# Index scores with ScalarE weighing a head in every second unit, and the row statistics of the second and fourth layernorm at the ends of the attentions

## The chip, the cores and the metric

The kernel runs on one core of one Trainium2 chip, as one launch. The core has TensorE (PE in the profile: matmuls and transposes), VectorE (DVE), ScalarE (ACT), GpSimd (POOL) and SyncE (SP, which issues most DMAs). Each works through its own list of instructions in order, and they meet by semaphores. SBUF holds the tensors, 128 partitions wide; PSUM holds the matmul results in 8 banks of 512 fp32 columns. The metric is the device time of the launch in microseconds.

## What is computed

One block of a model with 2048 tokens of width 256: x goes through a layernorm and attention A, a layernorm and a mixture of experts, a layernorm and attention B, a layernorm and the same experts again. Attention A has a mask made of index scores, which is where the first part of the change lies:

```python
x = x + attn_a(layernorm(x)); x = x + ffn(layernorm(x))
x = x + attn_b(layernorm(x)); x = x + ffn(layernorm(x))

# the index scores in attn_a, HI = 4 heads of DI = 64
dots = relu(einsum('bqhd,bkhd->bhqk', qi, ki))
index_scores = einsum('bhqk,h->bqk', dots, idx_w)
thr = the adaptive_k-th largest of each row of index_scores
top_k_mask = index_scores >= thr

def layernorm(x, eps=1e-5):
    m = mean(x, -1); v = var(x, -1)
    return (x - m) / sqrt(v + eps)
```

## The kernel before

**Stages.** The program is a row of blocks with a barrier of all engines at each block's end: ln1, preparation of the index, then for each half of the queries (group, g = 0 and 1) the index scores and the threshold search, preparation of A, attention A, ln2, experts, ln3, preparation of B, attention B, ln4, experts. Between the barrier of one stage and the first work of the next, GpSimd clears semaphores. The order inside a stage is written out by hand, for each engine a list.

**Index scores** (`index_scores`). A group has 8 tiles of 128 queries, and each tile two halves of 1024 keys: 16 units. A unit has four heads. For a head TensorE makes 128x1024 dot products by four matmuls into one of four pairs of PSUM banks (L454), ScalarE takes the relu into `relu[:, h, :]` in SBUF (L477; in the profile this tile is called `x`, as its area is shared), and VectorE weighs and adds it into `scores`: the first head by a multiplication (L499), the other three by a fused multiply and add (L502). There is one relu buffer a head, so that the relu of unit u waits until VectorE has used that of unit u - 1 (semaphore `summed`), and TensorE's matmuls of unit u wait for the relu of unit u - 1 (`relu_done`). The queries of the second 512 columns are projected in between: after heads number 5, 10, 15 and 20 of the 64 (table `LATER`), TensorE makes a projection (L430), ScalarE keeps its high part (L467) and VectorE its low part (L487).

**Layernorm** (`layernorm`). VectorE takes sixteen row statistics of x, one for each tile of 128 rows (L147, in a loop of four times four), then eight small instructions on 128x16, ScalarE a square root (its function table is loaded at the block's start), VectorE a reciprocal, and then it normalizes tile after tile (L168), TensorE transposes each (L217) and ScalarE stores it (L183). ln2 and ln4 also make the router's logits (L200), which wait for the router's seven loads, issued by SP at the block's start. ln3 gets its statistics ready made: in the experts VectorE takes them (L2371) right behind the last additions to x.

**End of attention A** (`attention_a`). GpSimd adds each head's output to x (L1239), the last pair for tile 15. VectorE's last work there is splitting transposed probabilities (L1425).

**End of attention B** (`attention_b`). For each tile VectorE takes the reciprocal of 16 sums (L1916), multiplies (L1925), TensorE transposes (L1832), ScalarE stores (L1887), TensorE multiplies with the output weights (L1807), and VectorE adds the result to x (L1919), five tiles behind the products (`LATE` = 5).

Of the kernel before, what the change touches and what calls it, by code (L numbers as in the profile page):

```python
# [11 lines left out]
ALU = mybir.AluOpType  # L12
# [369 lines left out]
def index_scores(nc, tag, g, xT, psum, w_q, b_q, q_stack, k_stack, k_lo, q_alone, relu, weight, scores, high, low):  # L382
# [4 lines left out]
    UNITS = GT * HALVES  # L387
    LATER = {HI * (1 + j) + j + 1: HI + j for j in range(HI * (QC - 1))}

    def pair(h):  # L390
        return psum[:, h * WIDE:(h + 1) * WIDE]

    with Phase(nc, tag) as phase:
# [9 lines left out]
        summed = sem("summed")  # L403
        with nc.Block() as block:
# [58 lines left out]
            def _(act):  # L463
# [8 lines left out]
                for u in range(UNITS):  # L472
                    for h in range(HI):
                        act.wait_ge(dotted, u * HI + h + 1)
                        if u:
                            act.wait_ge(summed, (u - 1) * HI + h + 1)
                        nc.scalar.activation(relu[:, h, :], pair(h), ACT.Relu).then_inc(relu_done, 1)  # L477
                        if u * HI + h in LATER:
                            keep_high(LATER[u * HI + h])

            @block.vector
            def _(dve):
# [10 lines left out]
                for u in range(UNITS):  # L493
                    t, half = divmod(u, HALVES)
                    into = scores[:, t, half * WIDE:(half + 1) * WIDE]
                    for h in range(HI):
                        dve.wait_ge(relu_done, u * HI + h + 1)
                        if h == 0:
                            nc.vector.tensor_scalar(into, relu[:, h, :], weight[:, 0:1], None, ALU.mult).then_inc(summed, 1)  # L499
                        else:  # L500
                            dve.wait_ge(summed, u * HI + h)
                            nc.vector.scalar_tensor_tensor(out=into, in0=relu[:, h, :], scalar=weight[:, h:h + 1], in1=into,  # L502
# [609 lines left out]
def attention_a(nc, arg, x, xT, bank, const, k_hi, k_lo, c_stack, bias, w_out, nowhere, q_rows):  # L1112
# [15 lines left out]
    with Phase(nc, "aa") as phase:  # L1128
# [60 lines left out]
        with nc.Block() as block:  # L1189
# [211 lines left out]
            def _(dve):  # L1401
# [50 lines left out]
                walk(dve, before, run, dve_order)  # L1452

# [153 lines left out]
def attention_b(nc, arg, x, xT, psum, bank, const, stash, q_stack, k_stack, zeroed, staged, stashed, same_in, after, halves, values):  # L1607
# [51 lines left out]
    with Phase(nc, "ab") as phase:  # L1659
# [9 lines left out]
        inv = [sb(f"inv{p}", [P, HB, 1]) for p in range(DEEP)]  # L1669
# [26 lines left out]
        with nc.Block() as block:  # L1696
# [194 lines left out]
            def _(dve):  # L1891
# [21 lines left out]
                for t in range(NT + LATE):  # L1913
                    p = t % DEEP
                    if t < NT:
                        nc.vector.reciprocal(inv[p][:], o_sums[:, t, :, DHB:]).then_inc(inv_done, 1)  # L1916
                    if t >= LATE:
# [3 lines left out]
                    if t < NT:  # L1921
                        dve.wait_ge(inv_done, t + 1)
# [651 lines left out]
```

## Time and profile before

| | us |
|---|---|
| median of three timed runs | 2668.33 (2663.47 to 2684.12) |
| the profiled execution's own time | 2662.5 |
| its span, first to last instruction | 2660.6 |
| TensorE busy | 2288.9 (86%) |
| VectorE busy | 1791.9 (67%) |
| ScalarE busy | 1673.3 (63%) |
| GpSimd busy | 723.1 (27%) |
| 128 relus of the index scores (L477) | 125.1 |
| 16 + 16 row statistics of ln2 and ln4 | 5.33 and 5.32 |

Busy shares are averages over stages with different limits. In the timeline a row is one instruction or several equal ones in a row (x3), with its start, the time from the first start to the last end, its engine and line, what it writes and reads, and in brackets how long the engine stood idle ahead of it and what ended that. Instructions of one engine can overlap by a little. SPq is SP's DMA issue. "PEq L98" as a releaser is a barrier.

### The profile page before, as it was taken

The page shows a single profiled execution, that of the slowest core. Times are in us where ns is not written, and L with a number is a line of the kernel's source. Part 1 is how long each engine was busy: PE and PEld are TensorE (multiplying, and loading weights), DVE is VectorE, ACT ScalarE, POOL GpSimd, SP SyncE. Part 2 cuts the span into 40 slices and gives each one's busy share as a digit, 9 for nine tenths or more (in the row PEclk, how much of TensorE's full clock was granted, in tenths as well). Part 3 has the DMA queues.
Part 4 walks back from the last instruction along what each step waited for, and adds up shares of the span by engine and source line. Part 5 has one row for each costly group of instructions (what it writes and reads, how often), then busy time and mean ns, then how long its engine had stood idle before and what let it go on. Part 6 is the DMA issues. An engine that isn't in the chain of part 4 may idle for free. (4 is left out here: it accounts for less than half of the span.)

```text
span 2660.6 us, 41889 instructions
## 1 busy us (share of the span) xinstructions
PE 2288.9 (86%) x12536; PEld 1556.2 (58%) x12536; DVE 1791.9 (67%) x3724; ACT 1673.3 (63%) x3045; POOL 723.1 (27%) x992
## 2 busy tenths in 40 slices
PE   6956595568999999999999999799569999997995
PEld 3633363347878787877787788465335444434663
DVE  4888798875777677767776777532568778744523
ACT  3779587946777777777777777323217777774232
POOL 0215411543321432143225422046220000100163
PEclk9978797878999999999999999899769999998998
DMA  1011102131000000000000000412360101000124
GB/s 50 1 40 63 64 1 74 56 127 44 21 13 13 22 21 13 13 26 17 13 13 25 17 1 1 128 58 84 97 195 1 49 2 49 2 1 4 52 88 142
DMA packets 77559, 113.14 MB, mean 43 GB/s; under 512 B 23860, under 2 KB 51860, under 8 KB 74644
## 3 DMA queue, kind: packets, MB, share of 16 engines
q1 hardware_dynamic: 66776, 89.55, 10.7%
q0 software_dynamic: 10560, 20.86, 2.6%
q8 instruction: 110, 1.80, 0.3%
q14 instruction: 113, 0.93, 0.1%
HBM read 67.25 MB, written 39.58 MB: 40 GB/s over the span
## 5 line engine op out<-in xcount | busy, mean ns | idle before, releaser
L1425 DVE TENSOR_TENSOR aa_pt_lo<-psum,aa_pt_hi 128x512 fp32r<-128x512 f32 x544 | 350.4, 685 | 82.8 <-ACT aa_pt_hi L1355 80.2
L1899 DVE TENSOR_REDUCE ab_part_max<-psum 128x2 f32<-128x1024 f32 (+3 forms) x320 | 327.0, 1062 | 93.9 <-PE psum L1745 92.0
L1355 ACT ACTIVATE aa_pt_hi<-psum 128x512 fp32r<-128x512 f32 x544 | 297.7, 598 | 116.0 <-PE psum L1285 113.1
L1847 ACT ACTIVATE ab_prob<-psum 128x512 f32<-128x512 f32 (+3 forms) x640 | 296.9, 541 | 100.3 <-PE psum L1774 96.5
L1412 DVE CUSTOM_DVE_ANT_0 aa_prob<-psum,bias 128x512 f32<-128x512 f32 (+2 forms) x480 | 278.6, 598 | 117.2 <-PE psum L1275 98.1
L1239 POOL TENSOR_TENSOR x<-aa_y_out,x 128x256 f32<-128x256 f32 x256 | 188.7, 737 | 353.0 <-ACT aa_y_out L1373 308.4
L1273 PE MATMUL psum<-ka_hi,aa_q_hi 128*128 128x512 f32 (+3 forms) x640 | 268.0, 419 | 10.8 <-POOL aa_q_lo L1207 8.0
L1285 PE MATMUL psum<-ident,aa_prob 128*128 128x128 f32 x1600 | 252.9, 274 | 6.8 <-issue 5.4
L1347 ACT ACTIVATE aa_prob<-aa_prob,aa_neg_max 128x128 f32<-128x128 f32 (+11 forms) x192 | 228.0, 1189 | 44.0 <-DVE aa_neg_max L1418 42.4
L1774 PE MATMUL psum<-b_q_stack,b_k_stack 64*128 64x512 f32 (+3 forms) x640 | 229.4, 432 | 15.3 <-ACT ab_prob L1847 10.7
L1296 PE MATMUL psum<-aa_pt_hi,c_stack 128*128 128x512 f32 x544 | 233.6, 429 | 5.9 <-ACT aa_out_t L1362 4.3
L1275 PE MATMUL psum<-ka_hi,aa_q_lo 128*128 128x512 f32 (+3 forms) x640 | 236.4, 369 | 0.0
L1274 PE MATMUL psum<-ka_lo,aa_q_hi 128*128 128x512 f32 (+3 forms) x640 | 236.0, 369 | 0.0
L1745 PE MATMUL psum<-b_k_stack,b_q_stack 63*128 63x512 f32 (+3 forms) x640 | 226.8, 468 | 6.7 <-DVE ab_part_max L1899 6.4
L1298 PE MATMUL psum<-aa_pt_lo,c_stack 128*64 128x512 f32 x544 | 215.4, 396 | 0.0
L1285 PEld LDWEIGHTS psum<-ident,aa_prob 128*128 128x128 f32 x1600 | 193.8, 141 | 30.2 <-issue 8.2
L1774 PEld LDWEIGHTS psum<-b_q_stack,b_k_stack 64*128 64x128 f32 x640 | 112.0, 189 | 107.8 <-ACT ab_prob L1847 91.3
L1207 POOL TENSOR_TENSOR aa_q_lo<-aa_q_row,aa_q_hi 128x512 fp32r<-128x512 f32 x64 | 82.6, 1291 | 332.5 <-ACT aa_q_hi L1339 332.5
L699 PE MATMUL psum<-ixt_w_heads,xT 128*128 128x512 f32 x256 | 133.9, 674 | 23.0 <-ACT ixt_w_heads L618 23.0
L1273 PEld LDWEIGHTS psum<-ka_hi,aa_q_hi 128*128 128x128 f32 x640 | 123.3, 193 | 49.1 <-DVE aa_chunk_max L1412 17.7
L1786 PE MATMUL psum<-ab_prob,b_values 128*17 128x512 f32 (+3 forms) x1280 | 149.7, 540 | 0.0
L1308 PE MATMUL psum<-wa_out,aa_out_t 128*128 (+1 forms) x512 | 135.3, 387 | 8.3 <-ACT aa_y_out L1373 4.3
(346 smaller groups left out, 4753.3 us busy)
## 6 DMA issues: line engine op xcount, KB each, us to landing
q_rows<-ixt_q_out SPq DMA_DIRECT2D x64, 256.0 KB, 2.0
aa_q_row<-q_rows SPq DMA_DIRECT2D x64, 256.0 KB, 2.6
f_back<-done SPq DMA_DIRECT2D x16, 512.0 KB, 8.0
w<-in_w SPq DMA_DIRECT2D x6, 896.0 KB, 9.6
x<-in_hidden SPq DMA_DIRECT2D x2, 2048.0 KB, 11.3
b_q_stack<-stash_q_hi SPq DMA_DIRECT2D x12, 256.0 KB, 4.2
b_k_stack<-stash_k_hi SPq DMA_DIRECT2D x12, 256.0 KB, 4.7
ixt_wq_n<-in_Wq_nope_T SPq DMA_DIRECT2D x2, 1024.0 KB, 5.3
```

The costliest lines, as they stand in the source:

```text
L1273: nc.tensor.matmul(out[:, 0:w], q_hi[t % 2][:, head], k_hi[:, cols], start=True, stop=False)
L1274: nc.tensor.matmul(out[:, 0:w], q_hi[t % 2][:, head], k_lo[:, cols], start=False, stop=False)
L1275: nc.tensor.matmul(out[:, 0:w], q_lo[t % 2][:, head], k_hi[:, cols], start=False, stop=True).then_inc(scores_ready, 1)
L1285: last = nc.tensor.transpose(turn_bank[(TB[t] + j) % RING][:, h * P:(h + 1) * P], prob[t % 2][h][:, j * P:(j + 1) * P], const["ident"][:])
L1296: nc.tensor.matmul(out[:], c_stack[:, j, :], pt_hi[ring][:], start=j == 0, stop=j == t, skip_group_check=True)
L1347: nc.scalar.activation(prob[t % 2][h][:, 0:L], prob[t % 2][h][:, 0:L], ACT.Exp, bias=neg_max[t % SUMS][:, h:h + 1], accum_out=total[t % SU ...
L1355: nc.scalar.activation(pt_hi[(TB[t] + j) % RING][:], turn_bank[(TB[t] + j) % RING], ACT.Copy).then_inc(pt_hi_done, 1)
L1412: nc.vector.tensor_tensor_reduce(prob[t % 2][h][:, c * CH:c * CH + w], score_bank[(QB[t] + h * chunks[t] + c) % 2][:, 0:w], bias[:, TRI[t] ...
L1425: nc.vector.tensor_tensor(pt_lo[ring][:], turn_bank[(TB[t] + j) % RING], pt_hi[ring][:].bitcast(F32), ALU.subtract).then_inc(pt_lo_done, 1)
L1774: nc.tensor.matmul(out[:, 0:w], k[at, kb * P:(kb + 1) * P], q[at, q0:q0 + w], start=not diag, stop=True, skip_group_check=True).then_inc(t ...
L1847: nc.scalar.activation(prob[i % 2][h][:, 0:w], t_bank[slot % RING][:, 0:w], ACT.Exp).then_inc(t_taken, 1)
L1899: nc.vector.tensor_reduce(part_max[e % 2][:, at:at + 5:4, part], s_pair[pair % 2][:, :, 0:w], AX.X, ALU.max).then_inc(s_used, 1)
```

## The change

**Index scores.** In units with an odd number ScalarE weighs the first head: behind the relu of head 1 it writes `relu[:, 0, :]` times the weight into `scores` (a Copy with a pointer scale) and increments a new semaphore `weighed`. VectorE has no L499 in these units; its first L502 waits for `weighed`. In even units all is as before. The relu of head 0 in an even unit waits for `weighed` and not for VectorE, and the counts of `summed` are those of VectorE's 7 instructions a pair.

**Layernorms 2 and 4.** The tile `stats` is allocated at the program's start. VectorE takes the sixteen row statistics at the end of attention A, each behind GpSimd's last addition to that tile, and at the end of attention B inside the loop over tiles, one tile behind the addition. ln2 and ln4 get `stats` and leave theirs out. In attention B one reciprocal of all 256 sums, in place, stands ahead of the loop and takes the place of the sixteen.

```diff
+    DVE_SUMS = 2 * HI - 1
+        def sums(u, h):
+            return DVE_SUMS * (u // 2) + (HI if u % 2 else 1) + h
...
                         act.wait_ge(dotted, u * HI + h + 1)
-                        if u:
-                            act.wait_ge(summed, (u - 1) * HI + h + 1)
+                        if u % 2 == 0 and u and h == 0:
+                            act.wait_ge(weighed, u // 2)
+                        elif u:
+                            act.wait_ge(summed, sums(u - 1, h))
                         nc.scalar.activation(relu[:, h, :], pair(h), ACT.Relu).then_inc(relu_done, 1)
+                        if u % 2 and h == 1:
+                            act.wait_ge(relu_done, u * HI + 1)
+                            nc.scalar.activation(into(u), relu[:, 0, :], ACT.Copy, scale=weight[:, 0:1]).then_inc(weighed, 1)
...
-                        dve.wait_ge(relu_done, u * HI + h + 1)
                         if h == 0:
-                            nc.vector.tensor_scalar(into, relu[:, h, :], weight[:, 0:1], None, ALU.mult).then_inc(summed, 1)
+                            if u % 2 == 0:
+                                dve.wait_ge(relu_done, u * HI + 1)
+                                nc.vector.tensor_scalar(into(u), relu[:, 0, :], weight[:, 0:1], None, ALU.mult).then_inc(summed, 1)
                         else:
-                            dve.wait_ge(summed, u * HI + h)
+                            dve.wait_ge(relu_done, u * HI + h + 1)
+                            if u % 2 and h == 1:
+                                dve.wait_ge(weighed, u // 2 + 1)
+                            else:
+                                dve.wait_ge(summed, sums(u, h - 1))
...
                 walk(dve, before, run, dve_order)
+                for t in range(NT):
+                    dve.wait_ge(x_added, ((NG - 1) * NT + t + 1) * GH + 4 * GH)
+                    nc.vector.bn_stats(stats[:, t, :], x[:, t, :])
...
                 dve.wait_ge(t_taken, SLOTS_USED)
-                for t in range(NT + LATE):
+                nc.vector.reciprocal(o_sums[:, :, :, DHB:], o_sums[:, :, :, DHB:]).then_inc(inv_done, 1)
+                dve.wait_ge(inv_done, 1)
+                for t in range(NT + LATE + 1):
                     p = t % DEEP
-                    if t < NT:
-                        nc.vector.reciprocal(inv[p][:], o_sums[:, t, :, DHB:]).then_inc(inv_done, 1)
-                    if t >= LATE:
+                    if LATE <= t < NT + LATE:
                         dve.wait_ge(out_done, t - LATE + 1)
                         nc.vector.tensor_tensor(x[:, t - LATE, :], x[:, t - LATE, :], out_bank[(t - LATE) % DEEP][:, 0:D],
                                                 ALU.add).then_inc(x_done, 1)
                     if t < NT:
-                        dve.wait_ge(inv_done, t + 1)
                         if t >= DEEP:
                             dve.wait_ge(o_turned, t - DEEP + 1)
                         nc.vector.tensor_tensor(o[p].rearrange("p (h d) -> p h d", d=DHB), o_sums[:, t, :, 0:DHB],
-                                                inv[p][:].to_broadcast([P, HB, DHB]), ALU.mult).then_inc(o_done, 1)
+                                                o_sums[:, t, :, DHB:].to_broadcast([P, HB, DHB]), ALU.mult).then_inc(o_done, 1)
+                    if t > LATE:
+                        dve.wait_ge(x_done, t - LATE)
+                        nc.vector.bn_stats(stats[:, t - LATE - 1, :], x[:, t - LATE - 1, :])
```

ScalarE's list at the start of the index scores before (L467 keeps a projection, L477 is a relu):

```order
L467 ACTIVATE ix_q_stack<-psum,ix_b_q 128x512 x4
L477 ACTIVATE x<-psum 128x1024 x6
L467 ACTIVATE ix_q_stack<-psum,ix_b_q 128x512
L477 ACTIVATE x<-psum 128x1024 x5
L467 ACTIVATE ix_q_stack<-psum,ix_b_q 128x512
L477 ACTIVATE x<-psum 128x1024 x5
L467 ACTIVATE ix_q_stack<-psum,ix_b_q 128x512
L477 ACTIVATE x<-psum 128x1024 x5
L467 ACTIVATE ix_q_stack<-psum,ix_b_q 128x512
L477 ACTIVATE x<-psum 128x1024 x43
```

and with the change (line numbers of the changed kernel: L477 keeps a projection, L489 is a relu, L492 the new copy):

```order
L477 ACTIVATE ix_q_stack<-psum,ix_b_q 128x512 x4
L489 ACTIVATE x<-psum 128x1024 x6
L492 ACTIVATE ix_scores<-x,ix_weight 128x1024
L477 ACTIVATE ix_q_stack<-psum,ix_b_q 128x512
L489 ACTIVATE x<-psum 128x1024 x5
L477 ACTIVATE ix_q_stack<-psum,ix_b_q 128x512
L489 ACTIVATE x<-psum 128x1024 x3
L492 ACTIVATE ix_scores<-x,ix_weight 128x1024
L489 ACTIVATE x<-psum 128x1024 x2
L477 ACTIVATE ix_q_stack<-psum,ix_b_q 128x512
L489 ACTIVATE x<-psum 128x1024 x5
L477 ACTIVATE ix_q_stack<-psum,ix_b_q 128x512
```

The first copy (unit 1) stands directly ahead of the keeping of a projection, the second and third (units 3 and 5) ahead of further relus.

VectorE's list around the end of attention A and the start of ln2 before (the loop has four statistics; the first stands here):

```order
L1433 RECIPROCAL aa_inv<-aa_total 128x4
L1425 TENSOR_TENSOR aa_pt_lo<-psum,aa_pt_hi 128x512 x22
L1189 UNCONDITIONAL_BRANCH
L141 UNCONDITIONAL_BRANCH
L144 UNCONDITIONAL_BRANCH
L144 ISA
L147 ISA
L147 BN_STATS ln_stats<-x 128x6
L147 ISA
```

and with the change:

```order
L1451 RECIPROCAL aa_inv<-aa_total 128x4
L1443 TENSOR_TENSOR aa_pt_lo<-psum,aa_pt_hi 128x512 x22
L1473 BN_STATS stats<-x 128x6 x16
L1207 UNCONDITIONAL_BRANCH
L141 UNCONDITIONAL_BRANCH
L151 TENSOR_TENSOR row_mean<-stats 128x16
L152 TENSOR_TENSOR ln_half<-stats 128x16
L153 TENSOR_TENSOR ln_var<-stats 128x16
L155 TENSOR_SCALAR row_mean<-row_mean 128x16
L156 TENSOR_SCALAR ln_half<-ln_half 128x16
```

The sixteen row statistics stand ahead of the end of the attention's block (its branch) now, and ln2 starts without the loop L144.

VectorE's list at the end of attention B before, from the reciprocal of the fourth tile on:

```order
L1916 RECIPROCAL ab_inv<-ab_o_sums 128x16
L1925 TENSOR_TENSOR xT<-ab_o_sums,ab_inv 128x256
L1916 RECIPROCAL ab_inv<-ab_o_sums 128x16
L1925 TENSOR_TENSOR xT<-ab_o_sums,ab_inv 128x256
L1916 RECIPROCAL ab_inv<-ab_o_sums 128x16
L1919 TENSOR_TENSOR x<-x,psum 128x256
L1925 TENSOR_TENSOR xT<-ab_o_sums,ab_inv 128x256
L1916 RECIPROCAL ab_inv<-ab_o_sums 128x16
L1919 TENSOR_TENSOR x<-x,psum 128x256
```

and with the change, from the start of that part:

```order
L1933 RECIPROCAL ab_o_sums<-ab_o_sums 128x256
L1944 TENSOR_TENSOR xT<-ab_o_sums 128x256 x5
L1939 TENSOR_TENSOR x<-x,psum 128x256
L1944 TENSOR_TENSOR xT<-ab_o_sums 128x256
L1939 TENSOR_TENSOR x<-x,psum 128x256
L1944 TENSOR_TENSOR xT<-ab_o_sums 128x256
L1948 BN_STATS stats<-x 128x6
L1939 TENSOR_TENSOR x<-x,psum 128x256
L1944 TENSOR_TENSOR xT<-ab_o_sums 128x256
L1948 BN_STATS stats<-x 128x6
```

The reciprocals of 16 columns are gone from between the products, one of 256 columns stands ahead, and a row statistic follows each addition to x by a product.

## Rows read from the trace of the kernel before

**Rows 1.** busy time by stretch, index stage: us, PE, PEld, DVE, ACT, POOL, clock

```profile
105.00:145.00 40.00, 37.63 (x144) 24.68 (x142) 37.50 (x33) 33.50 (x34) 6.33 (x7) 1.00 0.00 1
...
150.00:183.00 33.00, 9.33 (x35) 8.08 (x36) 28.94 (x56) 24.98 (x26) 0.00 (x0) 0.50 0.25 80
```

**Rows 2.** timeline of VectorE, index scores: start us, us, engine

```profile
115.95 0.75 DVE L499 TENSOR_SCALAR ix_scores<-x,ix_weight 128x1024 f32<-128x1024 f32 x1
116.80 4.07 DVE L502 SCALAR_TENSOR_TENSOR ix_scores<-x,ix_weight,ix_scores 128x1024 f32<-128x1024 f32 x3
120.78 0.90 DVE L499 TENSOR_SCALAR ix_scores<-x,ix_weight 128x1024 f32<-128x1024 f32 x1
121.79 4.06 DVE L502 SCALAR_TENSOR_TENSOR ix_scores<-x,ix_weight,ix_scores 128x1024 f32<-128x1024 f32 x3
```

**Rows 3.** timeline of ScalarE and TensorE in the index scores

```profile
71.63 5.62 ACT L477 ACTIVATE x<-psum 128x1024 f32<-128x1024 f32 x6 [2.31 <-PE psum L454]
...
119.57 1.03 ACT L477 ACTIVATE x<-psum 128x1024 f32<-128x1024 f32 x1 [0.36 <-DVE ix_scores L502]
...
117.21 0.73 PE L454 MATMUL psum<-ix_k_stack,ix_q_stack 128*128 128x512 f32 x2 [0.20 <-ACT x L477]
```

**Rows 4.** timeline of ScalarE in the first six units

```profile
85.90 0.69 ACT L467 ACTIVATE ix_q_stack<-psum,ix_b_q 128x512 fp32r<-128x512 f32 x1 [1.16 <-PE psum L430]
86.83 4.82 ACT L477 ACTIVATE x<-psum 128x1024 f32<-128x1024 f32 x5 [0.24 <-PE psum L454]
...
92.81 0.69 ACT L467 ACTIVATE ix_q_stack<-psum,ix_b_q 128x512 fp32r<-128x512 f32 x1 [1.15 <-PE psum L430]
```

**Rows 5.** groups of ScalarE by form: count, then busy us, mean ns

```profile
L1347 ACT ACTIVATE aa_prob<-aa_prob,aa_neg_max 128x1024 f32<-128x1024 f32 x8 | 9.2, 1151 | 0.2
```

**Rows 6.** timeline, end of the first attention and ln2

```profile
1674.63 1.52 POOL L1239 TENSOR_TENSOR x<-aa_y_out,x 128x256 f32<-128x256 f32 x2 [1.28 <-ACT aa_y_out L1373]
...
1678.56 0.41 SPq L2446 DMA_DIRECT2D f_gate_w<-in_gate_w  x1
...
1678.91 5.33 DVE L147 BATCH_NORM_STATS2 ln_stats<-x  x16 [10.70 <-PEq L98]
...
1686.00 5.26 DVE L168 TENSOR_SCALAR xn_first<-x,row_mean,row_rstd 128x256 f32<-128x256 f32 x16
```

**Rows 7.** timeline, start of ln3, whose row statistics come with x

```profile
1901.36 0.37 SPq L2495 DMA_DIRECT2D pb_w_dkv<-in_b_dkv_T  x1
...
1903.20 5.96 DVE L168 TENSOR_SCALAR ln_xn<-x,row_mean,row_rstd 128x256 f32<-128x256 f32 x16
```

**Rows 8.** timeline, end of the second attention and ln4

```profile
2414.86 0.25 DVE L1916 RECIPROCAL ab_inv<-ab_o_sums 128x16 f32<-128x16 f32 x1 [50.90 <-ACT ab_o_sums L1870]
...
2416.39 0.43 DVE L1925 TENSOR_TENSOR xT<-ab_o_sums,ab_inv 128x256 f32<-128x256 f32 x1
...
2422.76 0.42 DVE L1919 TENSOR_TENSOR x<-x,psum 128x256 f32<-128x256 f32 x1 [0.16 <-PE psum L1807]
...
2423.85 0.42 DVE L1919 TENSOR_TENSOR x<-x,psum 128x256 f32<-128x256 f32 x1 [0.17 <-PE psum L1807]
...
2435.33 0.42 DVE L1919 TENSOR_TENSOR x<-x,psum 128x256 f32<-128x256 f32 x1 [0.44 <-PE psum L1807]
...
2438.51 0.38 SPq L2446 DMA_DIRECT2D f_gate_w<-in_gate_w  x1
...
2445.94 5.26 DVE L168 TENSOR_SCALAR xn_second<-x,row_mean,row_rstd 128x256 f32<-128x256 f32 x16
```

**Rows 9.** groups of VectorE by form

```profile
L1433 DVE RECIPROCAL aa_inv<-aa_total 128x4 f32<-128x4 f32 x64 | 11.4, 178 | 35.8 <-ACT aa_prob L1347 30.4 <-issue 4.4
```

**Rows 10.** last router load of ln2: issue, landing, its reader

```profile
1681.42 0.43 SPq L2452 DMA_DIRECT2D f_trash<-in_trash  x1
...
f_trash<-in_trash SPq DMA_DIRECT2D x1, 19.5 KB, 2.8
...
1690.08 3.09 PE L200 MATMUL psum<-xT,f_gate_w 128*8 128x512 f32 x4
```

More of the change, by code:

```diff
@@ L403, in index_scores, with into @@
         summed = sem("summed")
+        weighed = sem("weighed")
+        def sums(u, h):
+            return DVE_SUMS * (u // 2) + (HI if u % 2 else 1) + h
+        def into(u):
+            t, half = divmod(u, HALVES)
+            return scores[:, t, half * WIDE:(half + 1) * WIDE]
         with nc.Block() as block:
@@ L493, in _ @@
                 for u in range(UNITS):
[L494 to L495 removed]
                     for h in range(HI):
[L497 removed]
                         if h == 0:
[L499 to L502 removed]
+                            if u % 2 == 0:
+                                dve.wait_ge(relu_done, u * HI + 1)
+                                nc.vector.tensor_scalar(into(u), relu[:, 0, :], weight[:, 0:1], None, ALU.mult).then_inc(summed, 1)
+                        else:
+                            dve.wait_ge(relu_done, u * HI + h + 1)
[3 more added lines that the diff above has]
+                                dve.wait_ge(summed, sums(u, h - 1))
+                            nc.vector.scalar_tensor_tensor(out=into(u), in0=relu[:, h, :], scalar=weight[:, h:h + 1], in1=into(u),
                                                            op0=ALU.mult, op1=ALU.add).then_inc(summed, 1)
@@ L1604, in same_rows, with attention_b @@
                                         same[row:row + 1, which, :]).then_inc(same_in, 16)
-def attention_b(nc, arg, x, xT, psum, bank, const, stash, q_stack, k_stack, zeroed, staged, stashed, same_in, after, halves, values):
+def attention_b(nc, arg, x, xT, psum, bank, const, stash, q_stack, k_stack, zeroed, staged, stashed, same_in, after, halves, values, stats):
     NG = HB // GB
@@ L2473, in load @@
                 load_experts(sp)
-            layernorm(nc, "ln2", x, xT, bank, const["ident"], mean, rstd, xn, router["gate_w"], router_in[0], bank[7], load)
+            layernorm(nc, "ln2", x, xT, bank, const["ident"], mean, rstd, xn, router["gate_w"], router_in[0], bank[7], load, stats)
             experts(nc, "f1", x, xT, xn, bank, const, router, w13, w2, shared_in, routed_in, rows, done, stats=stats)
@@ L2501, in program @@
                           after, halves, values)
-            attention_b(nc, arg, x, xT, psum, bank, const, stash, q_stack, k_stack, zeroed, staged, stashed, same_in, after, halves, values)
+            attention_b(nc, arg, x, xT, psum, bank, const, stash, q_stack, k_stack, zeroed, staged, stashed, same_in, after, halves, values, stats)
         with ExitStack() as f:
@@ L2508, in load @@
                 load_router(sp, router, router_in[1])
-            layernorm(nc, "ln4", x, xT, bank, const["ident"], mean, rstd, xn, router["gate_w"], router_in[1], bank[7], load)
+            layernorm(nc, "ln4", x, xT, bank, const["ident"], mean, rstd, xn, router["gate_w"], router_in[1], bank[7], load, stats)
             experts(nc, "f2", x, xT, xn, bank, const, router, w13, w2, shared_in, routed_in, rows, done, store=out)
```

7 lines of the change are left out of this document (3 added, 4 removed).

## The prediction

> **What bounds the kernel now.** The kernel is one core working through stages with barriers between them, so I read the busy times by stretch first, and then the timelines of the three places that the change touches; a shorter stage moves everything behind it forward, as long as nothing with a clock of its own (a load, TensorE's granted clock) is waited for. In the index scores VectorE works 37.50 of 40 us, ScalarE 33.50, TensorE 37.63 at granted clock 1.00, 2.4 GHz [rows 1]. TensorE's share is not what bounds it: it waits for ScalarE [rows 3], and ScalarE waits 0.36 us for VectorE ahead of a relu [rows 3], while VectorE's rows follow one another without idle time [rows 2]. A unit (four heads of a 128x1024 tile) starts at 115.95 and the next at 120.78: 4.83 us, all VectorE. At the ends of the attentions the chain is: the last addition to x, a barrier, sixteen row statistics on VectorE, nine small instructions, then the rows are normalized [rows 6, 8].
>
> **Index scores, units 6 to 15 of each of the two groups.** Every second unit loses L499 on VectorE. What goes is the distance from the start of L499 to the start of the first L502: 0.85 us (115.95 to 116.80) or, where L499 takes 0.90, 1.01 us (120.78 to 121.79) [rows 2]. Five pairs of units give 5 x 0.85 = 4.25 to 5 x 1.01 = 5.05; I take 4.65. ScalarE must be able to keep up. Six relus in a row take 5.62 and one alone 1.03, so they start (5.62 - 1.03) / 5 = 0.92 apart [rows 3]; eight are 7.4 us. A pair of units on VectorE will take 2 x 4.83 - 0.85 = 8.81, so there is 1.4 us of room for the copy. The trace has no Copy from SBUF of this size. The lower bound is the relu's 0.92, the upper the exponential of 128x1024 from SBUF with a pointer operand, 1.15 [rows 5]; I take 1.05, and either end fits into the room. The copy also stands ahead of the first L502 of its unit. It follows the second relu of the unit, which starts once VectorE has finished the first L502 of the unit before; VectorE then runs two more L502, 4.06 x 2 / 3 = 2.7 us [rows 2], against 0.92 + 1.15 = 2.1 us for relu and copy at most. So the wait for `weighed` costs nothing there. What is queued behind the copy are the relus of heads 2 and 3, and they have 1.4 us to spare per pair.
>
> The Trainium skill speaks against such a move: "ScalarE: Activation LUTs", section Rules for kernel authors, says to use VectorE for a multiplication. Its section What ACT_TABLE_LOAD costs gives 280 + 0.833 x 1024 = 1133 ns for such an instruction with one pointer operand, as an estimate. No run here shows that form yet; with 1.13 for 1.05 the sum would move by less than 0.2 us. The rule is about one instruction's time, while the rows show ScalarE with time over.
>
> **Units 0 to 5.** Here it is otherwise. Four projections of queries stand between the relus, ScalarE waits 1.15 us for each, and between two of them it works through: 85.90 to 92.81 holds its 0.69, five relus and the next wait [rows 4]. Three copies fall into this stretch. That of unit 1 stands directly ahead of such a wait, for a projection that doesn't hang on it: free. Those of units 3 and 5 lengthen ScalarE's chain, at 0.92 to 1.15 each: 1.8 to 2.3, and all three are free at best (0). I take 1.8. A group gains 4.65 - 1.8 = 2.85 us, two groups 5.7. Bounds of a group: 4.25 - 2.3 = 1.9 and 5.05 + 1.0 (if VectorE's relief counts there too) = 6.
>
> **Row statistics of ln2.** With the statistics known the layernorm starts as ln3 does: 1901.36 (SP's first issue in the block) to 1903.20 (first normalized tile) is 1.84 us [rows 7]. ln2 takes 1678.56 to 1686.00, 7.44 us [rows 6]. That is 5.60 less, of which the 5.33 of the sixteen instructions is the most. They go into the end of the attention, where VectorE is idle for 10.70 us ahead of the barrier [rows 6]: fifteen find x finished and are hidden in that gap, one comes after POOL's last addition, at 1674.63 + 1.52 = 1676.15. It adds some 0.1 of wait and 0.4 of its own (5.33 / 16 = 0.33 from start to start). The barrier took 2.41 us from POOL's end, and 2.76 from VectorE's at the second attention (2435.75 to 2438.51) [rows 6, 8]; VectorE ends last now, so 0.35 more. Net 5.60 - 0.5 - 0.35 = 4.7 us. If the cover is gone (fifteen instructions not hidden) the term is nothing.
>
> **Row statistics of ln4.** The same 5.60 (2438.51 to 2445.94 is 7.43) less 0.5 for the last instruction: 5.1. But the reciprocals change as well. Sixteen of 16 columns, 0.25 us each, become one of 256 columns ahead of everything. A reciprocal of 4 columns takes 178 ns [rows 9], one of 16 takes 0.25 [rows 8]: (0.25 - 0.178) / 12 = 6 ns a column, so 256 columns take 0.25 + 240 x 0.006 = 1.7 us. At the rate of a plain 128x256 instruction it would be 0.42 [rows 8]; those are the bounds, and I take 1.65. TensorE's first output tile hangs on the third product, at 2416.39 today. Then it starts at 2414.86 + 1.65 + 0.1 + 2 x 0.34 = 2417.29, since products without a reciprocal between follow closely: 0.9 us later (with 0.42 it is 0.3 earlier). From there the loop goes by TensorE: additions to x are 1.09 us apart and wait 0.16 for it [rows 8]. VectorE puts a row statistic (5.33 / 16 = 0.33) in the place of a reciprocal (0.25) into each step, and has the 0.16: hidden, just. If it weren't, 11 steps would cost up to 0.1 each. Net 5.1 - 0.9 = 4.2 us; bounds 3 and 5.4.
>
> The slope says that a reciprocal doesn't go at one column per cycle. The Trainium skill, "VectorE: DVE Perf Modes", section First, the fixed hardware budget, gives the division a repeat count of 8. At its clock of 0.96 GHz that would be an estimate of 2.1 us for 256 columns and 0.5 us off the sum; the slope of the rows is below it.
>
> **The sum.** 5.7 + 4.7 + 4.2 = 14.6 us, 0.55%. The span of the profiled execution is 2660.6 and its own time 2662.5; less 14.6 that is 2647.9. The three timed runs have the median 2668.33, which would give 2653.7. The median of all four executions is 2665.9, so I forecast 2665.9 - 14.6 = 2651.
>
> **Rivals.**
> A: ScalarE becomes the bound of the index scores. For: it gets a ninth instruction per pair, and units 0 to 5 are its chain already. Against: 1.4 us of room. It decides once the copy costs over 1.4, or copy and relu don't overlap; then the index part gives about nothing, 2657. TensorE gives the same outcome: 37.63 / 144 x 16 = 4.2 us per unit [rows 1] against the 4.4 wanted.
> B: the router's loads are waited for in ln2 and ln4. The last is issued at 1681.42 and lands 2.8 later, 5.7 us after the block starts; its first reader starts at 1690.08 [rows 10], 11.5 after, and then 11.5 - 5.6 = 5.9 after. It just fits. If the loads came 2 us late, 2 us go in each, 2655.
> C, slower: TensorE's low clock falls on the scores. It is at 0.50 (1.2 GHz) from 150 to 183, just behind the first group's scores [rows 1]. A unit needs 8.4 us of TensorE there, not 4.4. It decides from 31 us of such overlap (31 x (1 - 4.4 / 8.4) = 14.8); 33 us in each group are +31, 2682. Against: the stretch begins as the scores' last matmuls are done, and the scores now end earlier.
> D: the change does nothing that can be seen in the attentions, because the instructions wait for x to the end and the barrier is late by as much: 2665.9 - 5.7 = 2660.
> E: more than the sum: units 0 to 5 gain too, the reciprocal is cheap, and TensorE's idle time ahead of ln2 and ln4 is short enough to keep its clock up: 6 + 6 + 4.9 + 5.4 + some 3 = 25, 2641.
>
> **How the numbers follow.** Forecast 0.64, A 0.13, B 0.06, C 0.03, D 0.06, E 0.08. The forecast's own bounds (1.9 to 4 per group, 3.8 to 5.1 and 3 to 5.4) are 10.6 to 18.5 us, 2647 to 2655; the timed runs spread from 2663.47 to 2684.12, which widens it. The range takes in A, B, D and most of E: 2641 to 2663. About 1% (27 us) is what a measurement of this kernel can tell from no change. Faster by more needs all of E and a little of the spread: 0.09. Slower by more needs C or a disturbed median: 0.03. Within 1%: 0.88.
>
> **What would show it.** Right: VectorE's pairs of units 8.8 us apart from unit 6 on, units 3 and 5 later than before; copies of 1.0 to 1.15; SP's first issue to the first normalized tile 1.9 us in ln2 and ln4; fifteen row statistics ahead of POOL's last addition; one reciprocal of 1.65; additions to x still 1.09 apart. Wrong: VectorE waiting for the copy in late units (A), a gap of TensorE ahead of the first gate product (B), clock 0.50 inside the scores (C), additions to x over 1.15 apart.

## The result and the profile after

The changed kernel takes 2649.62 us (median of 20 runs, 2643.90 to 2668.33) against 2666.40 us for the kernel before (20 runs, 2659.59 to 2685.44). The ratio is 0.9929 with a 95% interval of 0.9910 to 0.9949: 0.7% faster. That is less than the kernel's own spread from run to run, but the interval lies below 1. The forecast was 2651. The lowest runs are 15.7 us apart, the medians 16.8, the sum of the forecast was 14.6. The profiled execution, however, has a span of 2654.4 us, only 6.2 less than the 2660.6 of before, so its stages have to be gone through one by one.

**Index scores.** The timeline of VectorE in the kernel after, behind unit 6 (L513 is the multiplication of an even unit, L520 the multiply and add; six L520 in a row are an even and an odd unit):

```profile
108.56 0.75 DVE L513 TENSOR_SCALAR ix_scores<-x,ix_weight 128x1024 f32<-128x1024 f32 x1
109.41 8.17 DVE L520 SCALAR_TENSOR_TENSOR ix_scores<-x,ix_weight,ix_scores 128x1024 f32<-128x1024 f32 x6
117.50 0.74 DVE L513 TENSOR_SCALAR ix_scores<-x,ix_weight 128x1024 f32<-128x1024 f32 x1
```

A pair of units takes 117.50 - 108.56 = 8.94 us, with no idle time of VectorE; before it was 4.83 + 4.98 = 9.81. ScalarE in the same stretch (L489 is a relu, L492 the copy):

```profile
117.68 3.08 ACT L489 ACTIVATE x<-psum 128x1024 f32<-128x1024 f32 x3 [0.26 <-DVE ix_scores L520]
120.65 1.14 ACT L492 ACTIVATE ix_scores<-x,ix_weight 128x1024 f32<-128x1024 f32 x1
121.69 4.67 ACT L489 ACTIVATE x<-psum 128x1024 f32<-128x1024 f32 x5
```

The copy takes 1.14 us, and 1.04 from its start to the next one's; ScalarE still waits 0.26 for VectorE, so it isn't the bound here. In the first six units it is. The timelines of ScalarE and VectorE around unit 3's copy, which answer to [rows 4]:

```profile
86.11 0.69 ACT L477 ACTIVATE ix_q_stack<-psum,ix_b_q 128x512 fp32r<-128x512 f32 x1 [1.16 <-PE psum L440]
87.04 3.05 ACT L489 ACTIVATE x<-psum 128x1024 f32<-128x1024 f32 x3 [0.24 <-PE psum L464]
89.99 1.14 ACT L492 ACTIVATE ix_scores<-x,ix_weight 128x1024 f32<-128x1024 f32 x1
91.03 1.93 ACT L489 ACTIVATE x<-psum 128x1024 f32<-128x1024 f32 x2
94.12 0.69 ACT L477 ACTIVATE ix_q_stack<-psum,ix_b_q 128x512 fp32r<-128x512 f32 x1 [1.16 <-PE psum L440]
...
91.23 4.06 DVE L520 SCALAR_TENSOR_TENSOR ix_scores<-x,ix_weight,ix_scores 128x1024 f32<-128x1024 f32 x3 [1.85 <-ACT ix_scores L492]
```

From one kept projection to the next it is now 94.12 - 86.11 = 8.01 us, where it was 6.91, and VectorE stands idle for 1.85 us until the copy is done. The first L502 or L520 of unit 6 starts 37.52 us after the first relu, 2.15 later than before (35.37).

**ln2.** The timeline of the end of attention A and the start of ln2, answering to [rows 6]:

```profile
1661.70 4.98 DVE L1473 BATCH_NORM_STATS2 stats<-x 128x6 f32<-128x256 f32 x15
1669.74 0.43 DVE L1473 BATCH_NORM_STATS2 stats<-x 128x6 f32<-128x256 f32 x1 [3.05 <-POOL x L1257]
...
1668.18 1.52 POOL L1257 TENSOR_TENSOR x<-aa_y_out,x 128x256 f32<-128x256 f32 x2 [1.26 <-ACT aa_y_out L1391]
...
1672.52 0.41 SPq L2468 DMA_DIRECT2D f_gate_w<-in_gate_w  x1
...
1674.36 5.25 DVE L168 TENSOR_SCALAR xn_first<-x,row_mean,row_rstd 128x256 f32<-128x256 f32 x16
...
1678.43 2.29 PE L200 MATMUL psum<-xT,f_gate_w 128*8 128x512 f32 x4
```

Fifteen row statistics end three microseconds ahead of the last addition to x, the sixteenth 0.47 behind it. From the block's start to the first normalized tile it is 1.84 us (7.44 before). The gate product starts as soon as the transposes are done, so the router's loads are not waited for.

**ln4.** The same for the end of attention B, answering to [rows 8]:

```profile
2410.91 1.76 DVE L1933 RECIPROCAL ab_o_sums<-ab_o_sums 128x256 f32<-128x256 f32 x1 [54.71 <-ACT ab_o_sums L1890]
2412.70 1.76 DVE L1944 TENSOR_TENSOR xT<-ab_o_sums 128x256 f32<-128x256 f32 x5
2416.53 0.42 DVE L1939 TENSOR_TENSOR x<-x,psum 128x256 f32<-128x256 f32 x1 [2.07 <-PE psum L1827]
...
2423.14 0.42 DVE L1939 TENSOR_TENSOR x<-x,psum 128x256 f32<-128x256 f32 x1
...
2424.22 0.42 DVE L1939 TENSOR_TENSOR x<-x,psum 128x256 f32<-128x256 f32 x1
...
2432.45 0.42 DVE L1939 TENSOR_TENSOR x<-x,psum 128x256 f32<-128x256 f32 x1
...
2436.28 0.38 SPq L2468 DMA_DIRECT2D f_gate_w<-in_gate_w  x1
...
2438.29 2.03 DVE L168 TENSOR_SCALAR xn_second<-x,row_mean,row_rstd 128x256 f32<-128x256 f32 x6
```

The reciprocal of 256 columns takes 1.76 us. The last addition to x ends 21.99 us behind the last sums, 20.93 before. Steps are 1.08 us apart as before.

**Where the profiled execution lost time.** The busy times by stretch (us; busy PE, PEld, DVE, ACT, POOL; clock; DMA share; GB/s) of all of attention B and its preparation, from ln3's first normalized tile to the last sums, before

```profile
1903.20:2414.80 511.60, 467.61 (x3792) 226.46 (x3792) 350.56 (x373) 336.96 (x733) 59.46 (x103) 0.94 0.14 41
```

and after:

```profile
1892.50:2410.90 518.40, 475.02 (x3792) 229.78 (x3792) 350.61 (x373) 337.30 (x733) 59.27 (x103) 0.92 0.14 41
```

The instructions of this stretch are the same in both kernels. It took 6.8 us more at a mean granted clock of 0.92 for 0.94. Attention A is not edited either, but for the row statistics behind it. From ScalarE's first instruction on `aa_prob` to GpSimd's last addition to x it took less than before. The same view, before

```profile
626.50:1676.20 1049.70, 1022.33 (x5690) 824.78 (x5690) 755.28 (x2141) 768.00 (x1438) 333.72 (x558) 0.99 0.06 16
```

and after:

```profile
622.70:1669.70 1047.00, 1020.23 (x5690) 826.36 (x5690) 760.29 (x2156) 767.62 (x1438) 332.97 (x558) 0.99 0.06 16
```

So the profile adds up as follows. The edited places give 13.6 us (below), and attention A 2.6. Attention B and its preparation take back 6.8, the two runs through the experts 0.9 and 1.5, and the other stages 0.9: 6.2 are left, within rounding. Whether the change has to do with the 6.8 is a question for the runs.

### The profile page after: what moved, and what is told of

Same layout as the page of the kernel before. It is cut to its first block and busy times, and to the rows that moved or that the text cites. A ratio compares the mean times of both kernels' runs of the same rounds, so it can differ in the third digit from the quotient of the medians.

```text
span 2654.4 us, 41782 instructions
## 1 busy us (share of the span) xinstructions
PE 2290.0 (86%) x12536; PEld 1560.5 (59%) x12536; DVE 1778.5 (67%) x3693; ACT 1684.8 (63%) x3061; POOL 721.3 (27%) x992
## 5 line engine op out<-in xcount | busy, mean ns | idle before, releaser
L717 PE MATMUL psum<-ixt_w_heads,xT 128*128 128x512 f32 x256 | 139.8, 700 | 22.8 <-ACT ixt_w_heads L636 22.8
L1291 PEld LDWEIGHTS psum<-ka_hi,aa_q_hi 128*128 128x128 f32 x640 | 123.3, 193 | 48.0 <-DVE aa_chunk_max L1430 17.1
```

The source lines that it names most:

```text
L1291: nc.tensor.matmul(out[:, 0:w], q_hi[t % 2][:, head], k_hi[:, cols], start=True, stop=False)
```

## The experiments

Each profile below was taken for itself. The index scores and the start of ln2 repeat in them to a tenth of a microsecond, so the size of such a part is read from its stage, and not from whole times. The loop at the end of attention B does not repeat so well, since TensorE's clock has a part in it: with the loop of before the last addition to x ends 20.93 us behind the last sums in two profiles and 21.96 in a third, where TensorE is at 1.2 GHz for the first 6.8 us of the loop. "Low stretch" below is a stretch in which TensorE is granted 1.2 GHz and not 2.4. A ratio is to the kernel before.

### The index part alone

```diff
 # kernel before, with index_scores of the changed kernel; ln2, ln4 and both attentions as before
```

> Only the index part of the change. Theory: each group's scores (first relu to last addition) 83.7 and 83.3 us before become 81.2, a loss of 2.1 us up to the first L502 of unit 6 and a gain of 4.7 behind it; ln2, ln4 and the end of attention B as before (7.44 us from SP's first issue to the first normalized tile); 4 to 5 us less time in all, ratio about 0.998. Rival (ScalarE is the bound everywhere): no gain behind unit 6. Rival (the small gain of the profiled execution is a cost of the change in attention B, from where stats lies in SBUF): here attention B, whose code and addresses are those of before, takes what it took before to 1 us; the theory is that TensorE's low clock falls there for a length that changes from execution to execution, so that attention B differs here by microseconds too.

Measured: 81.21 and 81.23 us a group (83.72 and 83.32 before), unit 6 at 37.5. ln2 and ln4 take 7.45 and 7.43. The ratio is 0.9965 (0.9934 to 0.9996). Attention B, with code and addresses of before, took

```profile
1892.10:2403.00 510.90, 467.22 (x3792) 226.04 (x3792) 350.40 (x373) 336.83 (x733) 59.46 (x103) 0.94 0.14 41
```

So the index part gives 4.6 us in its own stage, and ScalarE as the bound everywhere is out. The ratio stands for 9 us (1 to 18) where I expected 4 to 5. Attention A, not edited here, took 1046.7 us against 1049.6, which is another 2.9. On attention B this run alone decides nothing, since it had the length of before; the next ones do.

### The row statistics of ln2 alone

```diff
 # kernel before, with:
+                for t in range(NT):
+                    dve.wait_ge(x_added, ((NG - 1) * NT + t + 1) * GH + 4 * GH)
+                    nc.vector.bn_stats(stats[:, t, :], x[:, t, :])
 # behind walk() in attention_a, stats allocated at the start and handed to ln2
```

> Only the row statistics of ln2 at the end of attention A. Theory: fifteen of sixteen end ahead of GpSimd's last addition, the last ends 0.45 us behind it; SP's first issue of ln2 comes 2.8 us after GpSimd's end (2.4 before); the issue to the first normalized tile is 1.84 us (7.44 before); 5.2 us net up to the first tile. Rival (the router's loads become the wait): TensorE stands idle for 1 us or more between its first 16 transposes and the first gate product.

Measured: GpSimd ends at 1675.33, SP issues at 1678.15 (2.82 later), the first tile is normalized at 1679.99 (1.84). 7.44 - 1.84 - (2.82 - 2.41) = 5.2 us, as expected. This one execution took 2682.69 us in all, longer than the kernel before, and the reason stands in attention B, which is that of before:

```profile
1899.40:2434.00 534.60, 492.46 (x3792) 234.06 (x3792) 350.80 (x373) 337.80 (x733) 59.45 (x103) 0.88 0.14 39
```

23 us more at a clock of 0.88, with the same work on every engine. The clock's record shows where: TensorE is at half clock, 1.2 GHz, from 2372.6 for 68.3 us, where the profile of before has a stretch of 6.8 us at about the same place.

### The part in attention B and ln4 alone

```diff
 # kernel before, with the changed attention_b, and stats handed to ln4 but not to ln2
```

> Only the part in attention B and ln4. Theory: the reciprocal of 256 columns takes 1.75 us, the first addition to x comes 5.6 us after the start of the reciprocal (4.4 before) and the last 21.5 (20.5 before), and ln4 takes 1.85 to 2.0 us from SP's first issue to the first normalized tile (7.43 before): 3.7 us net. Rival (the row statistics between the additions slow the loop, and not the reciprocal its start): additions to x over 1.10 us apart from the fifth on, with VectorE without idle time, and the first addition no later than before.

Measured: the reciprocal 1.75 us, the first addition to x 5.39 us behind the last sums (4.47 before), the last ends at 22.27 (20.93 before), ln4 1.84 from issue to tile. From the last sums to the start of ln4 it is 25.67 (23.68). Net 7.43 - 1.84 - 1.99 = 3.6 us. From the start of the reciprocal the last addition ends at 22.24, where I expected 21.5; a low stretch covers the loop from 3.1 to 6.5 us behind the last sums. The timeline of VectorE in this run:

```profile
2422.19 1.75 DVE L1912 RECIPROCAL ab_o_sums<-ab_o_sums 128x256 f32<-128x256 f32 x1 [53.30 <-ACT ab_o_sums L1869]
2423.98 1.77 DVE L1923 TENSOR_TENSOR xT<-ab_o_sums 128x256 f32<-128x256 f32 x5
2427.55 0.42 DVE L1918 TENSOR_TENSOR x<-x,psum 128x256 f32<-128x256 f32 x1 [1.81 <-PE psum L1806]
```

The three parts alone give 4.6, 5.2 and 3.6 us: 13.4. The 3.6 is less certain than the other two, as the loop's length hangs on where the low stretch falls.

### The whole change with the small reciprocals

```diff
-                nc.vector.reciprocal(o_sums[:, :, :, DHB:], o_sums[:, :, :, DHB:]).then_inc(inv_done, 1)
-                dve.wait_ge(inv_done, 1)
                 for t in range(NT + LATE + 1):
                     p = t % DEEP
+                    if t < NT:
+                        nc.vector.reciprocal(inv[p][:], o_sums[:, t, :, DHB:]).then_inc(inv_done, 1)
...
```

> The whole change, but with the sixteen small reciprocals of before in attention B's loop, and the row statistics behind them. Theory (the late start is the large reciprocal's): the first addition to x is back at 4.4 us after the first reciprocal, but VectorE now has 0.28 more a step: 0.28 + 0.34 + 0.34 + 0.34 = 1.30 against TensorE's 1.09, so 11 steps lose 0.2 each and the last addition is at 22 to 23 us. Rival (VectorE's idle 0.16 covers it): additions stay 1.09 apart and the last is at 20.5 us.

Measured: the first addition is back at 4.47 us, so the late start was the large reciprocal's. But the last addition ends at 20.71, not at 22 to 23. My sum of a step was wrong and the rival right:

```profile
2409.13 0.42 DVE L1950 BATCH_NORM_STATS2 stats<-x 128x6 f32<-128x256 f32 x1
2409.47 0.24 DVE L1937 RECIPROCAL ab_inv<-ab_o_sums 128x16 f32<-128x16 f32 x1
2409.62 0.36 DVE L1940 TENSOR_TENSOR x<-x,psum 128x256 f32<-128x256 f32 x1
2409.90 0.41 DVE L1946 TENSOR_TENSOR xT<-ab_o_sums,ab_inv 128x256 f32<-128x256 f32 x1
2410.22 0.42 DVE L1950 BATCH_NORM_STATS2 stats<-x 128x6 f32<-128x256 f32 x1
...
2422.10 0.42 DVE L1940 TENSOR_TENSOR x<-x,psum 128x256 f32<-128x256 f32 x1
```

A reciprocal of 0.24 us lets the next instruction start after 0.15, and that one takes 0.28 to the next start. Four instructions make 2410.22 - 2409.13 = 1.09 us, TensorE's own pace. The row statistics would have been hidden without touching the reciprocals; hoisting them only cost 21.99 - 20.71 = 1.3 us between these two profiles (1.2 of it are there at the first addition, 5.65 against 4.47). Times here add up by starts, not by durations.

### ScalarE weighing from unit 7 on

```diff
+    BY_ACT = [u for u in range(UNITS) if u % 2 and u >= 7]
...
-                        if u % 2 and h == 1:
+                        if u in BY_ACT and h == 1:
```

> The whole change, but ScalarE weighs only in units 7, 9, 11, 13 and 15 of a group; units 1, 3 and 5 are as before. Theory: in units 0 to 5 ScalarE's chain with the projections is the bound and the copies lengthen it, so unit 6 starts where it did before (first L502 at 35.4 us after the first relu, 37.5 with the whole change), the gain behind it stays 4.7, and a group takes 79.1 us (81.2 with the whole change). Rival (the late start of unit 6 is a slower TensorE or DMA, not the copies): unit 6 is at 37.5 still.

Measured: unit 6 at 35.32 and 35.35 us, a group takes 79.00 and 79.03. VectorE's idle time ahead of unit 3's L520 is gone:

```profile
88.24 0.75 DVE L513 TENSOR_SCALAR ix_scores<-x,ix_weight 128x1024 f32<-128x1024 f32 x1
89.09 4.06 DVE L520 SCALAR_TENSOR_TENSOR ix_scores<-x,ix_weight,ix_scores 128x1024 f32<-128x1024 f32 x3
```

The ratio to the kernel before is 0.9887 (0.9848 to 0.9925). The copies of units 1, 3 and 5 together cost 2.2 us a group and are of no use there.

### ScalarE weighing in every unit from 7 on

```diff
-    BY_ACT = [u for u in range(UNITS) if u % 2 and u >= 7]
+    BY_ACT = [u for u in range(UNITS) if u >= 7]
```

> The whole change, but ScalarE weighs in no unit up to 6 and in every unit from 7 to 15. Theory: ScalarE has about 1.5 us of room a pair, and the second copy (1.05 from start to start) takes more than the 0.4 that the first has left: ScalarE needs 8 x 0.92 + 2 x 1.05 = 9.5 us a pair against VectorE's 8.0, and a pair takes 9.5 us where it takes 8.94 with the whole change (9.81 before); VectorE waits for ScalarE in each unit. Rival (VectorE is still the bound): a pair takes 8.0 to 8.3.

Measured: two units take 9.39 us (first L520 of unit 10 at 48.38, of 12 at 57.77), a group 80.97 and 80.67. VectorE waits in each unit:

```profile
113.88 4.06 DVE L520 SCALAR_TENSOR_TENSOR ix_scores<-x,ix_weight,ix_scores 128x1024 f32<-128x1024 f32 x3 [0.20 <-ACT ix_scores L492]
118.57 4.06 DVE L520 SCALAR_TENSOR_TENSOR ix_scores<-x,ix_weight,ix_scores 128x1024 f32<-128x1024 f32 x3 [0.63 <-ACT ix_scores L492]
```

That is rival A of the prediction beyond the point from which it decides: one copy a pair fits into ScalarE's room, the second makes ScalarE the bound. A group is hardly shorter than with the whole change (81.2), and longer than with one copy a pair from unit 7 on (79.0).

### The best of these together

```diff
+    BY_ACT = [u for u in range(UNITS) if u % 2 and u >= 7]
...
+                for e in range(EVENTS):
+                    g, c = divmod(e, NCH)
+                    dve.wait_ge(t_taken, SLOT[("flip", e)] + 1)
+                    sums = o_sums[:, 4 * c:4 * c + 4, g * GB:(g + 1) * GB, DHB:]
+                    nc.vector.reciprocal(sums, sums).then_inc(inv_done, 1)
                 dve.wait_ge(t_taken, SLOTS_USED)
-                nc.vector.reciprocal(o_sums[:, :, :, DHB:], o_sums[:, :, :, DHB:]).then_inc(inv_done, 1)
-                dve.wait_ge(inv_done, 1)
+                dve.wait_ge(inv_done, EVENTS)
```

> As the run that weighs from unit 7 on, and attention B's reciprocals are taken as sixteen pieces of 16 columns, each as soon as its sums are there, while VectorE is idle at the end of attention B. Theory: 14 or 15 of the pieces are hidden, the first product starts about 0.3 us after the last sums instead of 1.8, the last addition to x comes 1.2 to 1.5 us sooner than with the whole change; in all 5.5 us less than the whole change, ratio to the kernel before 0.991 to 0.992. Rival (the start of the loop goes by TensorE's low clock and not by the reciprocal): the last addition to x at the same distance from the last sums as with the whole change.

Measured: 2637.34 us (median of 6), ratio 0.9885 (0.9853 to 0.9917). In the timeline of VectorE fifteen pieces lie in idle time and one behind the last sums:

```profile
2340.30 1.70 DVE L1936 RECIPROCAL ab_o_sums<-ab_o_sums 128x16 f32<-128x16 f32 x14
2354.16 0.26 DVE L1936 RECIPROCAL ab_o_sums<-ab_o_sums 128x16 f32<-128x16 f32 x1 [12.16 <-ACT ab_o_sums L1890]
...
2401.09 0.26 DVE L1936 RECIPROCAL ab_o_sums<-ab_o_sums 128x16 f32<-128x16 f32 x1 [46.68 <-ACT ab_o_sums L1890]
2401.45 1.77 DVE L1948 TENSOR_TENSOR xT<-ab_o_sums 128x256 f32<-128x256 f32 x5
2404.07 0.42 DVE L1943 TENSOR_TENSOR x<-x,psum 128x256 f32<-128x256 f32 x1 [0.85 <-PE psum L1827]
```

The last addition ends 19.26 us behind the last sums: 2.7 sooner than with the whole change, twice what I expected, and 1.7 sooner than before. The first product starts 0.4 us behind the last sums, against 1.8 with the whole change: that is 1.4 of the 2.7. The other 1.3 are not VectorE's, since the five products follow each other without reciprocals in both kernels. They are TensorE's clock. Between TensorE's first transpose of the loop and the first addition to x lie 3.26 us with the whole change and 2.05 here. The busy times by stretch for this piece, with the whole change

```profile
2413.30:2416.50 3.20, 3.20 (x11) 2.71 (x12) 1.17 (x4) 1.15 (x3) 0.00 (x0) 0.50 0.00 0
```

and here:

```profile
2402.00:2404.00 2.00, 1.98 (x12) 1.54 (x13) 1.22 (x4) 0.99 (x3) 0.00 (x0) 1.00 0.03 8
```

In this execution TensorE had no low stretch in the loop. Whether that is chance or the edit's doing, one profile can't tell; I had not counted on it.

With 79.0 us a group the places add up to 4.7 + 4.3 + 5.2 + 5.6 + 1.7 - 0.7 = 20.8 us against the kernel before. The ratio says 30 us, with an interval of 22 to 39. In the profile a large part of the rest lies in attention A, which the edit leaves alone:

```profile
614.00:1656.70 1042.70, 1016.38 (x5690) 822.75 (x5690) 760.08 (x2157) 767.42 (x1438) 333.64 (x558) 0.99 0.06 16
```

It is 7.0 us shorter than before, and TensorE is busy 6.0 us less for the same 5690 instructions. The profile of the run that weighs from unit 7 on has 1042.7 us too. The eight profiles with an index part in the kernel have 1042.7 to 1047.0 us, the three without 1048.8 to 1049.6; two executions of the whole change differ by 1.7. Why is open. TensorE spends 22.1 us of it at 1.2 GHz instead of 29.0, which explains 3.5 us at most (an estimate: half of the difference).

### The whole change once more

> The whole change once more, on the same chip as the runs beside it. Theory: index scores 81.2 us a group again, ln2 and ln4 1.84 to 2.0 us from first issue to first tile; attention B and the experts differ from the first profile of it by microseconds, as TensorE's low clock lies elsewhere or lasts for another length. Rival (the change itself costs time in attention B): the same low stretch of 17 us ahead of the end of attention B again.

Measured: 2652.82 us (median of 12), ratio 0.9937 (0.9910 to 0.9965). Index scores 81.21 and 81.19 us, ln2 1.84, ln4 2.01. Attention B:

```profile
1885.60:2409.40 523.80, 481.50 (x3792) 230.59 (x3792) 350.76 (x373) 337.54 (x733) 59.46 (x103) 0.91 0.14 40
```

The same kernel took 518.4 us there in the first profile, and the low stretch that starts at 2356.3 lasts 37.5 us, where it lasted 17.1. At the end of attention B the last addition to x ended 23.28 us behind the last sums, 1.3 later than in the first profile, as TensorE was at 1.2 GHz for 6.8 us of the loop instead of 3.4. So the part in attention B and ln4 gave 2.4 us in this execution and not 3.7. Attention A took 1045.3 us.

All eleven profiles together. The second column says how far behind ln3's first normalized tile the low stretch begins, the third how long it is:

| profile | begins, us | low stretch, us | attention B, us |
|---|---|---|---|
| index part alone | 467.9 | 6.8 | 510.9 |
| small reciprocals | 468.2 | 6.8 | 511.7 |
| short copies (next section) | 468.2 | 6.8 | 511.6 |
| before | 468.6 | 6.8 | 511.6 |
| best | 469.1 | 34.1 | 521.3 |
| part in attention B alone | 470.3 | 13.7 | 515.0 |
| weighing from unit 7 on | 470.4 | 34.1 | 522.7 |
| after, second | 470.7 | 37.5 | 523.8 |
| every unit from 7 on | 470.8 | 68.3 | 532.3 |
| after, first | 472.9 | 17.1 | 518.4 |
| row statistics of ln2 alone | 473.2 | 68.3 | 534.6 |

The length of attention B follows the stretch and not the code: the longest is a kernel whose attention B is that of before, one of the shortest has the changed one. So the 6.8 us that the first profile lost are not a cost of the change. What the table shows beyond that: the four stretches that begin earliest, by 468.6 us, are all 6.8 us long, and the seven that begin later are 13.7 to 68.3. What sets the length among those was not found out.

The timed runs bear this out. Each has its mean granted clock on record, and a kernel's time follows it closely. At 0.928 the kernel before takes 2665.87 us (median of 5 runs) and the whole change 2652.64 (of 3), 13.2 less; at 0.923 it is 2679.48 and 2666.85 (3 and 3), 12.6 less. The median clock is 0.927 in 31 runs of before and 0.9315 in 32 of the whole change, so the change doesn't lower the clock. That it raises it isn't shown.

The kernels that ran once took 2682.69 us (row statistics of ln2), 2666.06 (part in attention B), 2643.67 (small reciprocals), 2663.16 (every unit from 7 on) and 2645.62 (short copies). With stretches of 68.3, 13.7, 6.8, 68.3 and 6.8 us, these times alone say nothing of the edits.

### Short copies on GpSimd

```diff
+                    n = P if t < 2 else 2
...
-                        nc.gpsimd.tensor_copy(q_alone[t % 2][rows, odd::2, :],
-                                              q_stack[rows, odd::2, t * P:(t + 1) * P].bitcast(F32)).then_inc(staged, 1)
+                        nc.gpsimd.tensor_copy(q_alone[t % 2][rows, odd::2, 0:n],
+                                              q_stack[rows, odd::2, t * P:t * P + n].bitcast(F32)).then_inc(staged, 1)
```

> The whole change, but from the third query tile on GpSimd copies 2 of 128 columns into q_alone, so the low part of the dot products uses old data there: the scores leave out that part of the computation. Theory: the 0.13 us by which a pair of units (8.94) is longer than the 8.81 forecast is one L502 (its line in the changed kernel: L520) of 1.42 us that runs beside GpSimd's copy, and the others of 1.28 do not; with short copies all take 1.28 and a pair from unit 6 to 13 takes 8.81. Rival (the 1.42 comes from what VectorE reads or from ScalarE's copy into scores beside it): the 1.42 stays, and a pair is at 8.94.

Measured: a pair takes 8.81 us (first additions of units 8, 10 and 12 at 46.21, 55.02 and 63.83), a group 80.67 and 80.69. The instructions that write the scores, min, median and max in ns, after

```profile
L520 DVE SCALAR_TENSOR_TENSOR ix_scores<-x,ix_weight,ix_scores x96: 1277/1284/1421, 73.9 to 408.8; 128x1024 f32<-128x1024 f32 x96
```

and with short copies:

```profile
L521 DVE SCALAR_TENSOR_TENSOR ix_scores<-x,ix_weight,ix_scores x96: 1277/1285/1287, 73.9 to 407.5; 128x1024 f32<-128x1024 f32 x96
```

The 1.42 us instruction is gone with the copies beside it. In the kernel before, the three multiplications of 0.89 to 0.90 us in each group (0.75 otherwise) are the ones that run beside such a copy. So the saving of 1.01 us in a unit that I read off 120.78 to 121.79 [rows 2] was only 0.85: the rest is GpSimd's, and 0.13 of it moved to another instruction.

## Why the prediction was right

**Bound and index scores, units 6 to 15.** VectorE was the bound and stayed it; ScalarE kept up with 0.26 us to wait. The copy's 1.14 us in duration is the upper end of the bounds (1.15), its 1.04 from start to start is the value taken. The Trainium skill's figure, "ScalarE: Activation LUTs", section What ACT_TABLE_LOAD costs, was 1133 ns by its formula: the trace agrees. The Trainium skill's rule to leave a multiplication to VectorE (the same page, section Rules for kernel authors) did not decide here. The gain was 4.7 us in the first group and 4.3 in the second for 4.65 forecast (44.30 to 39.62 and 43.92 to 39.61 us from unit 6 to unit 15). The first group of before holds a stall of 0.4 us of VectorE in unit 14 that isn't there after. Without that stall it is 4.3 in both groups, and the term was sized too high by what GpSimd's copies take.

**Units 0 to 5.** The mechanism was right, and its price 2.15 us where 1.8 was taken. Index part in all: 2.5 + 2.2 = 4.7 us for 5.7.

**ln2.** 5.60 less to the first tile, as ln3 had shown. The barrier took 2.82 us from GpSimd's end instead of 2.41, so 0.41 is the whole cost of the last row statistic: 5.2 us net for 4.7. The step that failed is the extra 0.35 for a barrier behind VectorE: from VectorE's end it was 1672.52 - 1670.17 = 2.35, less than the 2.76 read at attention B.

**ln4.** The slope of two small reciprocals gave 1.7 us for the large one, and it took 1.76. The last addition is 1.06 later for 0.9 forecast, and the row statistic adds 0.66 behind it for 0.5. In the first profile ln4's start took 2.01 us, so 7.43 - 2.01 - 1.06 - 0.66 = 3.7 us for 4.2; in the second it was 2.4. The prediction had VectorE alone set when the loop starts, and left out TensorE's clock there, which moves the end of the loop by 1.0 to 1.3 us in either kernel. The Trainium skill's repeat count of 8 ("VectorE: DVE Perf Modes", section First, the fixed hardware budget), as an estimate 2.1 us, is above what the trace shows.

**The sum** is 4.7 + 5.2 + 3.7 = 13.6 us for 14.6, with misses of -1.0, +0.5 and -0.5, and timed runs of equal clock differ by 12.6 and 13.2. The medians moved by 16.8. The prediction put every stage that is not edited at nothing. Attention A was 2.6 and 4.3 us shorter in the two profiles of the whole change, and attention B longer by 6.8 and 12.2. So the mechanism and the size of the terms were right, but that 2651 lies 1.4 from the median is luck.

**Rivals.** A did not come, and one run shows where it does. B did not come: the gate product follows the transposes without a gap. C did not come in the scores, but its mechanism, a low stretch of TensorE's clock of a length that nothing in the kernel fixes, made up to 23 us in attention B. It is a large part of the spread of whole times, and I had looked for it in the wrong stage. D is refuted by the fifteen hidden row statistics. E was wrong about units 0 to 5 and about a cheap reciprocal. Nor was the clock kept up ahead of ln2: the granted clock was 0.50 from the first normalized tile at 1674.36 to 1679.3, and from the same tile to ln3 it took 218.1 us, 217.2 before.

## What to carry to other kernels

Work given to another engine is free only where that engine waits: find the stretches in which it is part of a chain (here ScalarE, TensorE and the projections), and leave those out; that doubled the index part's gain. Take row statistics, reciprocals and the like as soon as their data are there, in a gap that the trace shows ahead of a barrier, and in pieces, since one large instruction behind the last input is a delay for all that follows. Add up an engine's steps by start to start. Judge a change of a few microseconds by its own stages when whole times spread by 25, but go through the stages that it leaves alone as well, and compare whole times at equal granted clock: here two stages that nobody had edited moved by up to 7 and up to 23 us.

## What the runs showed of the hardware that I had not expected

A reciprocal costs VectorE by its columns: 0.178 us for 4, 0.25 for 16, 1.76 for 256; but in a row of instructions one of 0.24 holds back the next by only 0.15. A copy of 64x256 by GpSimd that runs on for some 0.35 us into a 128x1024 instruction of VectorE lengthened it by 0.14 us (0.75 to 0.89 or 1.28 to 1.42). Not each overlap does so: in the kernel before, the multiply and add at 80.54 had 1.2 us of such copies beside it and took 1.29. TensorE was at 1.2 GHz for 6.8 to 68.3 us at nearly the same place of the same code in different executions (it fell 467.9 to 473.2 us behind ln3's first normalized tile), in the middle of work, and a stage of 511 us took up to 23 us more for it.
